# Attention with a masked numerator: softmax denominators of four key tiles partly pre-added on GpSimd and VectorE

## What is computed

```python
q = jnp.einsum('bsc,hcd->bhsd', xn, wq)
k = jnp.einsum('btc,hcd->bhtd', yn, wk)
v = jnp.einsum('btc,hcd->bhtd', yn, wv)
a = jax.nn.softmax(jnp.einsum('bhsd,bhtd->bhst', q, k) * D ** (-0.5), axis=-1)
if causal:
    s, t = (a.shape[-2], a.shape[-1])
    mask = (jnp.arange(t)[None, :] > jnp.arange(s)[:, None]).astype(a.dtype)
    a = a * mask
o = jnp.einsum('bhst,bhtd->bhsd', a, v)
```

## Time and profile before

| | us |
|---|---|
| median of 3 runs | 3277.24 (3270.82 to 3278.95) |
| the profiled execution | 3272.99 |
| its span, first to last instruction | 3271.3 |
| the stage of the change (us 1136 to 1524 of the span) | 388.0 |
| PE busy in it | 375.6 |
| POOL busy in it | 220.2 |
| ACT busy in it | 197.9 |
| DVE busy in it | 174.4 |

### The profile page before, as it was taken

One profiled execution on the slowest core, in us unless ns is written; L12 is line 12 of the kernel. 1 busy time (PEld: TensorE's weight loads), 2 busy tenths in 40 slices (PEclk: granted clock), 3 DMA queues, 4 the chain that ended last, 5 costly groups with the idle time before them and its releaser, 6 DMA issues. The chain is left out here.

```text
span 3271.3 us, 45479 instructions
## 1 busy us (share of the span) xinstructions
PE 2719.4 (83%) x17197; PEld 1564.1 (48%) x17204; DVE 1884.7 (58%) x3449; ACT 1468.2 (45%) x1978; POOL 1114.5 (34%) x996
## 2 busy tenths in 40 slices
PE   5888887779889799998868998798998997798544
PEld 3343433633346444445744444486777776233222
DVE  4655656577665444444556666644444443776688
ACT  1556557236632254455424555534333332366322
POOL 3233332213211355565235888520010111122334
PEclk7899998979989799999888999899999998799666
DMA  6566562065520011112000000002212112565100
GB/s 163 121 118 135 122 127 65 17 114 118 116 92 14 17 38 41 45 46 73 27 14 1 1 1 14 14 2 72 74 52 65 61 58 72 99 114 108 26 10 15
DMA packets 130376, 202.76 MB, mean 62 GB/s; under 512 B 36368, under 2 KB 66608, under 8 KB 129520
## 3 DMA queue, kind: packets, MB, share of 16 engines
q1 hardware_dynamic: 98416, 147.46, 19.4%
q0 software_dynamic: 31744, 52.41, 5.9%
HBM read 134.92 MB, written 64.78 MB: 61 GB/s over the span
## 5 line engine op out<-in xcount | busy, mean ns | idle before, releaser
L2366 DVE TENSOR_REDUCE L_mx<-bank_t 128x2 f32<-128x1024 f32 (+3 forms) x512 | 564.8, 1121 | 332.9 <-PE bank_t L2182 206.6
L2366 DVE TENSOR_REDUCE L2a_mx<-bank_t 128x2 f32<-128x1024 f32 x256 | 311.8, 1223 | 349.9 <-PE bank_t L2159 348.7
L2569 ACT ACTIVATE L_P<-bank_t 128x1024 f32<-128x1024 f32 (+3 forms) x384 | 340.5, 916 | 249.4 <-PE bank_t L2194 134.4
L2569 ACT ACTIVATE L2a_P<-bank_t 128x1024 f32<-128x1024 f32 x256 | 261.6, 1023 | 258.3 <-PE bank_t L2171 257.8
L2182 PE MATMUL bank_t<-L_KS,L_QS 48*128 48x512 f32 (+2 forms) x1024 | 238.0, 467 | 126.9 <-ACT L_P L2569 48.0
L2159 PE MATMUL bank_t<-L2a_QK 32*128 32x512 f32 x1536 | 257.3, 446 | 58.4 <-ACT L2a_P L2569 27.3
L2194 PE MATMUL bank_t<-L_QS,L_KS 50*128 50x512 f32 (+2 forms) x1024 | 243.7, 480 | 20.9 <-DVE L_mx L2366 12.8
L2167 PE MATMUL bank_t<-L2a_QK 32*128 32x512 f32 x1536 | 254.6, 442 | 0.0
L2159 PEld LDWEIGHTS bank_t<-L2a_QK 32*128 32x128 f32 x1536 | 139.6, 196 | 223.5 <-ACT L2a_P L2569 119.5
L2194 PEld LDWEIGHTS bank_t<-L_QS,L_KS 50*128 50x128 f32 x1024 | 100.3, 196 | 257.0 <-issue 168.0
L2224 PE MATMUL bank_o<-L_P,L_V 128*32 128x512 f32 (+3 forms) x1536 | 198.6, 592 | 8.4 <-ACT L_P L2569 6.1
(11 more groups left out here) (455 smaller groups left out, 5991.8 us busy)
## 6 DMA issues: line engine op xcount, KB each, us to landing
L_KS<-L_spill_k_halves SPq DMA_DIRECT2D x174, 128.0 KB, 5.6
L_QS<-L_spill_q_halves SPq DMA_DIRECT2D x174, 128.0 KB, 4.5
L_spill_raw<-xn POOLq DMA_DIRECT2D x64, 256.0 KB, 2.5
L2g_raw<-in_L_ffn_h_blocks SPq DMA_DIRECT2D x32, 512.0 KB, 3.7
L_spill_k_halves<-L_hi SPq DMA_DIRECT2D x32, 256.0 KB, 2.1
L_spill_k_halves<-L_lo SPq DMA_DIRECT2D x32, 256.0 KB, 2.3
L_spill_q_halves<-L_hi SPq DMA_DIRECT2D x32, 256.0 KB, 2.0
L_spill_q_halves<-L_lo SPq DMA_DIRECT2D x32, 256.0 KB, 3.3
```

Source lines behind the costliest of these rows:

```text
L2366: e.tensor_reduce(neg, s.tile[:, :, 0:n_keys], AX.X, ALU.max, negate=True).then_inc(sem(s.done), 1)
L2569: e.activation(s.at.Pr[s.pb][:, :, q0:S], s.tile[:, :, q0:S], ACT.Exp, scale=s.at.scale).then_inc(sem(s.exp), 1)
```

## The change

The key tiles go 0, 1, 2, 3. Only places 2 and 3 of a pair have products with ones: place 2 with its own probabilities, place 3 with the first tile's buffer, to which POOL has added the second tile's probabilities and DVE the fourth's (`AddPair`, 128 x 1024 float32 elements, in place, all operands in SBUF). The sum of both products is the sum over the four tiles. The first tile can be overwritten since key tile 0 has no value product but that of its masked block in `diag`. Each add is a delayed step: it comes into the plan one tick after its own tick, behind that tick's mask, scores, values and group copy. The ring of `P` becomes seven. The diff, cut to its core:

```diff
-            NP_ = 7 if pooled else 6
+            NP_ = 7 if D == 32 else 6
...
             def key_tiles(mode):
-                return [3, 2, 1, 0] if mode == "upper" else [0, 1, 2, 3]
+                return [0, 1, 2, 3]
...
+            ADDED, ALONE = {1: "gpsimd", 3: "vector"}, (2,)
+
+            def add_pair(first, part, by):
+                done = due("pair_added_" + by)
+                dst, src = at.Pr[first[0]][:, :, :], at.Pr[part[0]][:, :, :]
+                add(AddPair(dst, src, by, [part[1], first[1], first[3], pair_added.get(first[0])], done))
+                P_free[part[0]] = P_free[part[0]] + [done]
+                pair_added[first[0]] = done
...
-            def values(un, g, kt, place, parts):
+            def values(un, g, kt, place, parts, head=None):
...
+                sums_of, e_sum = None, None
+                if upper and place in ALONE:
+                    sums_of = parts[0][0], place == ALONE[0], False
+                elif upper and last:
+                    sums_of, e_sum = (head[0], False, True), pair_added.pop(head[0])
...
+                            elif upper and place == 0:
+                                head = parts[0]
+                            elif upper and place in ADDED:
+                                pair = lambda head=head, part=parts[0], by=ADDED[place]: add_pair(head, part, by)
+                                if at_tick == len(flat) - 1:
+                                    pair()
+                                else:
+                                    delayed.append((tick[0], pair))
...
-                            if s.at.GP == 1 and i == 0:
-                                mm = e.matmul(bank_o[row + 32:row + 64, :], ones[:, 0:32], s.at.Pr[pb][:, c, :],
-                                              start=s.first, stop=s.last, tile_position=(0, row + 32))
+                            if s.summed is not None and i == 0:
+                                whole, opens, closes = s.summed
+                                mm = e.matmul(bank_o[row + 32:row + 64, :], ones[:, 0:32], s.at.Pr[whole][:, c, :],
+                                              start=opens, stop=closes, tile_position=(0, row + 32))
...
+                elif kind is AddPair and s.by == "vector":
+                    dve.wait_ge(*s.after)
+                    e.tensor_tensor(s.dst, s.dst, s.src, ALU.add).then_inc(sem(s.done), 1)
...
+                elif kind is AddPair and s.by == "gpsimd":
+                    pool.wait_ge(pool.latest, *s.after)
+                    e.tensor_tensor(s.dst, s.dst, s.src, ALU.add).then_inc(sem(s.done), 1)
+                    pool.latest = s.done
```

More of the change, by code:

```diff
@@ L100 @@
 Logits = namedtuple("Logits", "at un s kt tile after mm pb exp_after exp")
-Values = namedtuple("Values", "at un g kt first last parts i_v after mm")
+Values = namedtuple("Values", "at un g kt first last parts i_v summed after mm")
+AddPair = namedtuple("AddPair", "dst src by after done")
 CopyGroup = namedtuple("CopyGroup", "at un g raw after done raw_dram den_dram out_after landing")
@@ L503, in attention @@
             sums_free, inv_free, summed, n_sums = [None] * 4, [None, None], {}, [0]
-            n_pair, n_group, n_diag = [0], [0], [0]
+            n_pair, n_group, n_diag, pair_added = [0], [0], [0], {}
             tick, delayed, chores, maxima, last_chore = [0], [], [], [], [-9]
@@ L727, in values @@
                 first, last = place == 0, place == TB - 1
-                add(Values(at, un, g, kt, first, last, parts, i_v, [e_v, *[p[1] for p in parts], *[p[3] for p in parts],
-                                                                    o_free[0] if first else None], mm))
+                sums_of, e_sum = None, None
[3 more added lines that the diff above has]
+                    sums_of, e_sum = (head[0], False, True), pair_added.pop(head[0])
+                add(Values(at, un, g, kt, first, last, parts, i_v, sums_of,
+                           [e_v, *[p[1] for p in parts], *[p[3] for p in parts], o_free[0] if first else None, e_sum], mm))
+                if e_sum is not None:
+                    P_free[head[0]] = P_free[head[0]] + [mm]
                 for pb, _, i_d, _ in parts:
@@ L867, in attention @@
                            [[step] for step in entry.side.rest()] + entry.later_steps()]
-            pending, at_tick = [], 0
+            pending, at_tick, head = [], 0, None
             for un in units:
@@ L898, in attention @@
                                     un, p, place, part)))
+                            elif upper and place == 0:
[6 more added lines that the diff above has]
+                                    delayed.append((tick[0], pair))
                             at_tick += 1
-                        pending.append(lambda un=un, g=g, kt=kt, place=place, parts=parts: values(
-                            un, g, kt, place, parts))
+                        pending.append(lambda un=un, g=g, kt=kt, place=place, parts=parts, head=head: values(
+                            un, g, kt, place, parts, head))
                 finished.add(un.n)
```

## The result

The changed kernel takes 3326.0 us (median of 4 runs, 3309.6 to 3329.4) against 3275.9 for the kernel before in the same measurement: the ratio is 1.0138, 95% interval 1.011 to 1.0166, about 45 us more (the medians are 50 apart). A repeat beside later experiments gave 1.0123 (1.0102 to 1.0143). The forecast was 3286 with a range of 3264 to 3296: the sign was right, the size and the range were not. The profiled execution has a span of 3325.2 us (before 3271.3).

What follows compares the result with a forecast made beforehand. Plain ticks were taken as bound by the 2.37 us loop of scores and DVE maxima, chore ticks by PE. Gains of 16.6 us against costs of 25.3 gave +8.7: 3281.7 profiled, 3286 as median, range 3264 to 3296.

Steps and rivals of the forecast that it cites:

- savings, ticks 0 to 111: Fewer products with ones shorten K and V projection ticks (4.7, 2.0), turnings (4.6) and four early turning ticks (1.4 us).
- waits on VectorE and GpSimd, ticks 8 to 111: Nine late subtractions cost 14.9 us, late maxima in next ticks 5.6, adds longer than DVE's idle gap about 1.
- What bounds a tick: Plain ticks follow the 2.37 us loop of scores and DVE maxima; PE bounds turning ticks (2.72) and projection ticks (4.04).
- The stall's place: Ticks 28, 36, 44, 60, 68, 76, 92, 100, 108: maxima 1.65 us late, in all 14.9.
- What stalls: DVE's subtraction of the maxima's parts waits 2.37 us for POOL's add instead of 0.75 for the mask.
- The 0.8 in the next tick: DVE's add waits for POOL's division, so the next tick's maxima begin 0.8 us late: 7 plain ticks, 5.6 us.
- DVE's adds and POOL's DMA issues: By the exclusive lock alone, DVE's additions would not hold up POOL's DMA issues; no row showed that pair.
- The clock stays 1.00: PE's granted clock in the stage stays at 1.00, the level of 2.4 GHz.
- The sum for the last twelve ticks: Without maxima, POOL needs 9.5 us per four ticks against PE's 7.4: 3.8 us of delay against 3.9 saved.
- the adds hide: Rival: adds fit into idle engine time, leaving 16.6 us gain less 1, 3261 to 3262; chance 0.17, wholly or mostly hidden.
- stalls in every pair: Rival: POOL falls behind and DVE's add also waits in ticks 8k: +21.5 us, 3299; chance 0.20, shared with less PE gain.

Runs made afterwards that it cites:

- e1: The changed kernel without any AddPair, key tiles 1 and 3 left out of the denominators: 3265.0 us, ratio 0.9966 to the kernel before.
- e9: The changed kernel with ten extra transposes on TensorE before its wait for the turned maxima, in ten units: 3313.2 us, ratio 1.0098 to the kernel before.
- e12: The changed kernel unaltered, run again beside later experiments: 3320.8 us, ratio 1.0123 to the kernel before.
- after: The changed kernel as first measured, with all its adds: 3326.0 us, ratio 1.0138 to the kernel before.
- e7: The changed kernel with no adds and products with ones at all four key tiles in the last two units: 3305.3 us, ratio 1.0084 to the kernel before.
- e4: The changed kernel with both adds of each pair on VectorE, none on GpSimd: ratio 1.0031 to the kernel before.
- e8: The changed kernel with VectorE's cast and subtraction of the row maxima replaced by memsets of zeros: 3292.3 us, ratio 1.0054 to the kernel before.

## Why the prediction was right and wrong

| Term | forecast | runs |
|---|---|---|
| savings, ticks 0 to 111 | -12.7 | -11.7 (e1) |
| waits on VectorE and GpSimd, ticks 8 to 111 | +21.5 | +22.2 (e9 less e1) |
| clock behind these waits | 0 | +11.7 to +16.6 (e12 and after, less e9) |
| last 15 ticks | -0.1 | +20.6 (after less e7) |

- *What bounds a tick* was right: loop 2.37, K ticks to 3.6, turnings to 2.37, all as put down. The claim that half of the 135.8 us of ones is worth little held: up to tick 111 it is worth 11.7 us, forecast 12.7. The difference is the ticks 3 and 4, which together took no less than before. The 3.9 of the last ticks weren't had; over the whole stage e1 is 8.1 shorter, not 16.6.
- *The stall's place* was right: ticks 28, 36, 44, 60, 68, 76, 92, 100 and 108, nine casts of 2.2 to 2.6. I had ruled out tick 12, and it stalls as well (3.42).
- *What stalls* was partly wrong. I let the subtraction alone wait for POOL's add and then win over the mask, and my rule named only instructions with two sources, although the cast of 2.19 in the earlier trace rows was against it. The cast waited already, and at eight of nine places the subtraction met the mask too. At full clock (e9) such a tick takes 4.57, for which I had 4.02: 2.20 above the loop instead of 1.65, 18.7 for the nine against 14.9.
- *The 0.8 in the next tick* wasn't there behind such a tick (2.40): the longer turning tick gave DVE time for its add. Where the subtraction slipped in before the mask (tick 68) both are as I had them: 3.97, and 3.02 in the next. The two ticks together are 6.97 and 6.99, so the two errors cancel, by luck: with the plain ticks behind them the nine stalls cost 19.5 in e9, forecast 20.5. Small losses in the ticks 12, 13, 52, 84 and 105 make 2.7 more, for which I had 1.
- *DVE's adds and POOL's DMA issues* don't hold each other up: in e4 two issues last their usual 0.61 and 0.56 (from 1149.84) while an add of DVE runs (1149.26 to 1150.85).
- **"The clock stays 1.00" is the first step that failed.** I carried the stalls at the durations of full clock. PE waits 1.55 to 1.58 us at seven of them, 1.15 at tick 108 and 0.99 at tick 68; at all but tick 68 the granted clock falls to 0.50, and the rows behind are at 1.2 GHz for one or two ticks. That is the +11.7 to +16.6 of the table.
- **The sum for the last twelve ticks is the second.** I reckoned POOL's load there against PE's and got 3.8 of delay against 3.9 of saving. Left out were the turning of tick 116, which still has its cast and subtraction; the half clock behind it, which in ticks whose bound is PE costs 1.75 each; and what is queued behind DVE's add, the next stage's normalisation. The runs have +20.6 there instead of -0.1. The saving of 3.9 wasn't to be had at all, since even without adds that normalisation comes too late for a faster PE (e1: +3.6).
- *The rivals*: "the adds hide" is out, "stalls in every pair" too (the second pair's stalls are one tick in 104). The range failed because all rivals had sizes taken at one clock, so none lay above 3299. That the time went up, as I had forecast, is owed to the stalls, whose cost I had nearly right; less the savings they make 10 of the 45 us.

## What to carry to other kernels

When an instruction is given to GpSimd, look for the smallest two-source or casting VectorE instructions that start beside it, and for what TensorE does behind them: 0.2 us of work became 2.6 us of wait, and the same add one half unit later cost nothing in the loop but for one tick. Price a wait that leaves TensorE idle at both levels of its clock, and price what follows it at 1.2 GHz too. At a stage's end read what stands in the in-order queues behind the new instruction, because there the next stage's work is what TensorE needs next.

## What the runs showed of the hardware

- A cast of 128 x 16 lasted 2.58 us beside a GpSimd add of 2.37 that began, by the records, 0.16 after it (changed kernel; the same at seven other places), and 0.18 beside a GpSimd mask of 0.75 that began 0.17 after it (kernel before). A memset of the same size lasted 0.07 beside the add (e8).
- One wait of 2.57 us ahead of matmuls that then kept PE busy left PE at 1.2 GHz for the rest of the stage (ticks 117 to 126), while behind the waits of 1.55 us in the loop it was back at 2.4 GHz after one or two ticks. A wait of 0.99 didn't lower the clock at tick 68, while in the second profile of the changed kernel waits of 0.98 to 1.01 lowered it at five of six places. What tells these apart wasn't tried.
- With ten transposes of 128 x 128 (1.31 us) in the wait the granted clock stayed at 2.4 GHz behind it, at all ten places (e9).
